# An MoE decoder layer kernel: gated results scattered to their tokens, plain loads in the last stage

## The reference

```python
x1 = _layernorm(x + attn_out, g1, be1)
gate_probs = jax.nn.softmax(x1 @ Wg + bg, axis=-1)
topk_p, topk_i = jax.lax.top_k(gate_probs, K)                 # K = 2 of E = 8
topk_p = topk_p / jnp.sum(topk_p, axis=-1, keepdims=True)
h = jax.nn.gelu(jnp.einsum('bsd,edf->bsef', x1, W1) + b1, approximate=False)
y = jnp.einsum('bsef,efd->bsed', h, W2) + b2
moe_out = sum over the two chosen experts of topk_p * y
return _layernorm(x1 + moe_out, g2, be2)
```

## Time and profile before

| | us |
|---|---|
| median of three runs | 1700.76 |
| lowest, highest | 1695.51, 1703.92 |
| the profiled execution, its own time | 1700.69 |
| its span in the profile | 1698.9 |
| PE, DVE, ACT, POOL busy | 1376.5, 1166.6, 872.7, 642.1 |
| stages one and two end (last scatter issued) | about 1386 |
| tile phase, first to last TensorE work | 1395 to 1566 |
| last stage, first gather to end | 1570 to 1699 |

### The profile page before, as it was taken

How to read it: one execution, slowest core, us unless ns; L and a number is a source line. 1 busy time by engine, 2 the same in 40 slices (tenths; PEclk the granted TensorE clock), 3 DMA queues, 4 the chain that set the end, 5 groups by cost and what they waited for, 6 DMA issues and landing times.

```text
span 1698.9 us, 46753 instructions
## 1 busy us (share of the span) xinstructions
PE 1376.5 (81%) x19192; PEld 1120.8 (66%) x19192; DVE 1166.6 (69%) x3279; ACT 872.7 (51%) x2058; POOL 642.1 (38%) x912
## 2 busy tenths in 40 slices
PE   6899999999859988988989899898997739998000
PEld 5788787888737766766767667676675528887000
DVE  4777887778666888877878787888887631100565
ACT  3556555665425765556566565665666514444000
POOL 6415335243052245433443525535223220000885
PEclk8899999999979999999999999999999959999555
DMA  9932221211110011000010100101000026665232
GB/s 342 381 99 73 66 69 59 87 58 40 61 50 8 9 27 38 25 22 13 24 33 12 40 11 24 36 12 30 21 8 27 14 93 202 202 202 154 62 90 71
DMA packets 114293, 123.04 MB, mean 72 GB/s; under 512 B 21920, under 2 KB 87456, under 8 KB 113824
## 3 DMA queue, kind: packets, MB, share of 16 engines
q1 hardware_dynamic: 107936, 107.46, 19.6%
q0 software_dynamic: 6144, 12.60, 2.6%
HBM read 65.49 MB, written 54.53 MB: 71 GB/s over the span
## 4 chain that ended last, share of the span: by engine, by line
PE 53%; DVE 24%; POOL 8%; ACT 7%; issue 5%; DMA 1%; SPq 1%; DVEq 0%; POOLq 0%; ACTq 0%
PE bank L1847 6%; PE bank L1714 5%; DVE P L1492 4%; PE bank L2101 4%; DVE gs L1491 4%; PE bank L2094 3%; POOL P L1046 3%; PE bank L1726 3%; PE bank L1699 3%; PE bank L1896 2%; PE bank L1970 2%; PE bank L1885 2%; PE bank L1935 2%; PE bank L1892 2%; PE bank L1908 2%
## 5 line engine op out<-in xcount | busy, mean ns | idle before, releaser
L1166 ACT ACTIVATE P<-P 128x512 f32<-128x512 f32 x256 | 160.1, 630 | 99.9 <-DVE P L1492 98.5
L1491 DVE TENSOR_REDUCE gs<-bank 128x8 f32<-128x512 f32 (+1 forms) x256 | 174.5, 682 | 43.2 <-PE bank L1699 21.3
L1714 PE MATMUL bank<-const,P 128*128 128x128 f32 x1152 | 177.2, 284 | 29.4 <-ACT P L1166 20.8
L1492 DVE TENSOR_TENSOR P<-bank,gs 128x512 f32<-128x512 f32 x256 | 177.1, 692 | 8.8
L1714 PEld LDWEIGHTS bank<-const,P 128*128 128x128 f32 x1152 | 130.5, 143 | 70.0 <-ACT P L1166 42.1
L1847 PE MATMUL bank<-XT,wb 128*128 128x256 f32 x512 | 138.2, 397 | 3.1 <-ACT PT L1077 1.2
L1046 POOL DMA_INDIRECT P<-rows_x,places x64 | 64.6, 1009 | 200.9 <-DMA rows_x<-R 183.4
L1172 ACT ACTIVATE PT<-bank 128x512 f32<-128x512 f32 x192 | 109.7, 594 | 51.1 <-PE bank L1714 49.8
L1649 DVE TENSOR_TENSOR R<-bank,Q 128x256 f32<-128x256 f32 x40 | 17.0, 425 | 164.0 <-PE bank L2101 164.0
L989 POOL TENSOR_TENSOR P<-P,gs 128x512 f32<-128x512 f32 x64 | 66.0, 1046 | 155.4 <-DVE gs L1528 154.9
L1263 ACT ACTIVATE PT<-bank,Q 128x256 f32<-128x256 f32 x160 | 67.4, 471 | 84.7 <-PE bank L2094 84.4
(11 more groups left out here) (264 smaller groups left out, 3564.5 us busy)
## 6 DMA issues: line engine op xcount, KB each, us to landing
Q<-in_wm SPq DMA_DIRECT2D x40, 578.0 KB, 3.8
rows_x<-blank SPq DMA_DIRECT2D x4, 4864.0 KB, 33.7
y_mid<-PT SPq DMA_DIRECT2D x16, 512.0 KB, 2.8
y_mid<-D SPq DMA_DIRECT2D x16, 512.0 KB, 2.8
X<-rows_x SPq DMA_DIRECT2D x40, 128.0 KB, 2.2
rows_x<-R SPq DMA_DIRECT2D x40, 128.0 KB, 2.6
wb<-in_wb SPq DMA_DIRECT2D x1, 4228.0 KB, 15.3
V<-in_ctxT SPq DMA_DIRECT2D x32, 128.0 KB, 3.0
```

Of the source, the lines that this page charges most:

```text
L1166: act.activation(P[s][:, i, :], P[s][:, i, :], ACT.Exp, scale=scale).then_inc(p.of(s), 1)
L1491: st2(dve.tensor_reduce(mx, v, AX.X, ALU.max))
L1492: dve.tensor_tensor(P[s][:, i, :].rearrange("p (g m) -> p g m", m=width), v, each(mx, width), ALU.subtract).then_inc(s_sub.of(s), 1)
L1714: last = pe.transpose(tile(banks[s][i], t), tile(P[s][:, i, :], t), ident)
```

## The change

Rows of `rows_x` grow from 128 to 132 numbers: the token's row number plus one, its first expert, g1 and g2 follow the state. A tile's weights get one more column, the expert's number. X1 becomes a view of the wider buffer XW. In the tile phase DVE works out from these columns, for each row of the tile, the gate that applies and the row of a new DRAM tensor `y_rows` for the result (first choices in one part, second ones in another, rows without a token to spare rows). It multiplies the result by the gate behind the add of b2, and GpSimd scatters it there with two indirect DMAs a tile. SP's store of the tile goes. In the last stage SP loads both results of a group with plain loads, GpSimd adds them, DVE adds x1; the multiplication by g2 is joined with the subtraction of the mean, the one by 1/sqrt with the addition of x; the last normalisation is ACT's. The written-out orders of stages three and four are new (`pool3` and `act4` are added). Steady `sp3` is now "tx" of tile k+1, then "tw" of tile k, and it begins with "tx" of tiles 2, 3, 1, 0 and then "tw" of 0, 1, 2, 3, while TensorE turns tiles 0, 2, 1, 3 before its first up. Steady `dve3` is mostly "tp" of tile k+2, then "ty" of tile k+1. In `pe3` the steps of three tiles are interleaved.

```diff
@@ constants, buffers, lanes
+WIDE = DIM + 4
+PART = SEQ * SEQ + 1
-WM, NWM = spans(("w1", 512), ("w2", 512), ("b1", 4), ("b2", 128))
+WM, NWM = spans(("w1", 512), ("w2", 512), ("b1", 4), ("b2", 128), ("eid", 1))
-        X1 = per_slot("X1", [128, T, DIM])
+        XW = per_slot("XW", [128, T, WIDE])
+        X1 = [XW[s][:, :, 0:DIM] for s in range(SLOTS)]
-        blank = sb("blank", [128, 512])
+        blank = sb("blank", [128, 4 * WIDE])
@@ SP, stages three and four
             def tile(j, s):
                 yield "tx"
                 if j:
                     sp.wait_ge(m_x_ps.of(s), m_x_ps.at(j - 1, s))
+                    sp.wait_ge(m_row.of(s), m_row.at(j - 1, s))
...
-                yield "ty"
-                sp.wait_ge(m_y.of(s), m_y.at(j, s))
-                to = sp.value_load(table[0:1, j * SLOTS + s, 0:1], min_val=0, max_val=XROWS - NT)
-                sp.dma_start(d["rows_x"][bass.ds(to, NT), :].rearrange("(t p) d -> p t d", p=128), R[s][:, :, :]).then_inc(tile_y[s], 16)
...
+            for s in range(SLOTS):
+                sp.wait_ge(m_gelu.of(s), m_gelu.at(ROUNDS - 1, s))
+                sp.wait_ge(tile_y[s], 16 * T * ROUNDS)
+            for s in range(SLOTS):
+                load_results(0, s)
             def finish(n, s):
+                if n + 1 < passes:
+                    yield "ly"
+                    sp.wait_ge(c_ln_mv.of(s), c_ln_mv.at(n, s))
+                    load_results(n + 1, s)
+                    load_last_x1(n + 1, s)
+                    yield "lx"
+                    sp.wait_ge(c_r2_mv.of(s), c_r2_mv.at(n, s))
+                    load_last_x(n + 1, s)
                 yield "out"
@@ POOL, stages three and four
-                        pool.indirect_dma_start(P4[s][:, k, 128 * t:128 * t + 128], None, d["rows_x"][:, :], bass.IndirectOffsetOnAxis(
-                            ap=places[:, (n * SLOTS + s) * T + t, k:k + 1], axis=0)).then_inc(gathered[s], 16)
+            def tile(j, s):
+                yield "sc"
+                pool.wait_ge(m_gated.of(s), m_gated.at(j, s))
+                for t in range(T):
+                    pool.indirect_dma_start(d["y_rows"][:, :], bass.IndirectOffsetOnAxis(
+                        ap=gidx[s][:, t, j % 2:j % 2 + 1], axis=0), R[s][:, t, :], None).then_inc(tile_y[s], 16)
+            def finish(n, s):
+                yield "su"
+                pool.wait_ge(last_y[s], 16 * 3 * (n + 1))
                 if n:
                     pool.wait_ge(c_ln_mv.of(s), c_ln_mv.at(n - 1, s))
+                pool.tensor_tensor(P4[s][:, 2, :], P4[s][:, 0, :], P4[s][:, 1, :], ALU.add).then_inc(c_sum.of(s), 1)
                 yield "n4"
                 root(n, s, c_ln_mv, c_ln_rstd, pool2, 0)
                 yield "n5"
-                root(n, s, c_r2_mv, c_ln_rstd, pool2)
+                pool.wait_ge(c_r2_mv.of(s), c_r2_mv.at(n, s))
+                apart(pool)
+                pool2(pool, pool.tensor_scalar(rstd[s][:, :], mv[s][:, :, 1], EPS, None, ALU.add))
+                pool2(pool, pool.tensor_tensor(rstd[s][:, :], rstd[s][:, :], power[:, 0:T], ALU.pow))
+                pool2(pool, pool.tensor_tensor(shift[s][:, :], mv[s][:, :, 0], rstd[s][:, :], ALU.mult))
+                pool.tensor_scalar(shift[s][:, :], shift[s][:, :], -1.0, None, ALU.mult).then_inc(c_ln_rstd.of(s), 1)
@@ ACT, stage four
+            def finish(n, s):
+                yield "n5"
+                act.wait_ge(c_ln_rstd.of(s), c_ln_rstd.at(n, s, use=1))
+                if n:
+                    act.wait_ge(written[s], 16 * n)
+                for t in range(T):
+                    last = act.activation(X1[s][:, t, :], R[s][:, t, :], ACT.Identity, bias=shift[s][:, t:t + 1], scale=rstd[s][:, t:t + 1])
+                last.then_inc(c_out.of(s), 1)
@@ DVE, place (stage two)
-                g1, g2 = gates[:, c0:c0 + T, 0], gates[:, c0:c0 + T, 1]
+                g1, g2 = XW[s][:, :, DIM + 2], XW[s][:, :, DIM + 3]
+                dve.tensor_scalar(XW[s][:, :, DIM], C("rowbase")[:, c0:c0 + T], 1.0 / NE, 1.0, ALU.mult, ALU.add)
                 dve.wait_ge(b_g_exp.of(s), b_g_exp.at(n, s))
+                dve.tensor_copy(XW[s][:, :, DIM + 1], idf[:, :, 0])
@@ DVE, stages three and four
             def tile(j, s):
+                yield "tp"
+                row, e1, g1, g2 = (XW[s][:, :, DIM + k] for k in range(4))
+                eid = part(wm[s], WM, "eid")
+                dve.wait_ge(tile_x[s], 16 * (j + 1))
+                dve.wait_ge(tile_w[s], 16 * (j + 1))
+                dve.scalar_tensor_tensor(small[s][:, 0, 0:T], e1, eid, g1, ALU.is_equal, ALU.mult)
+                dve.scalar_tensor_tensor(small[s][:, 1, 0:T], e1, eid, g2, ALU.not_equal, ALU.mult)
+                st2(dve.tensor_scalar(small[s][:, 2, 0:T], e1, eid, float(PART), ALU.not_equal, ALU.mult))
+                dve.tensor_tensor(small[s][:, 3, 0:T], small[s][:, 0, 0:T], small[s][:, 1, 0:T], ALU.add)
...
+                dve.tensor_copy(gidx[s][:, :, j % 2], small[s][:, 4, 0:T]).then_inc(m_row.of(s), 1)
                 yield "ty"
                 dve.wait_ge(m_down_ps.of(s), m_down_ps.at(j, s))
                 if j:
-                    dve.wait_ge(tile_y[s], 16 * j)
+                    dve.wait_ge(tile_y[s], 16 * T * j)
                 dve.tensor_tensor(R[s][:, :, :], tok(half(s, 0)), over(part(wm[s], WM, "b2"), T), ALU.add).then_inc(m_y.of(s), 1)
+                dve.wait_ge(m_y.of(s), m_y.at(j, s))
+                for t in range(T):
+                    ins = dve.tensor_scalar(R[s][:, t, :], R[s][:, t, :], small[s][:, 3, t:t + 1], None, ALU.mult)
+                ins.then_inc(m_gated.of(s), 1)
...
+                st2(dve.tensor_tensor(R[s][:, :, :], tok(P4[s][:, 2, :]), tok(lastx1[s]), ALU.add))
                 norm_stats(s, st2, c_ln_mv)
                 yield "n4"
                 y = tok(PT4[s][:, 0, :])
+                dve.wait_ge(c_ln_mv.of(s), c_ln_mv.at(n, s))
+                for t in range(T):
+                    ins = dve.scalar_tensor_tensor(y[:, t, :], R[s][:, t, :], mv[s][:, t, 0:1], Row("g2"), ALU.subtract, ALU.mult)
+                st2(ins)
                 dve.wait_ge(c_ln_rstd.of(s), c_ln_rstd.at(n, s, use=0))
+                dve.wait_ge(last_x[s], 16 * (n + 1))
+                for t in range(T):
+                    ins = dve.scalar_tensor_tensor(R[s][:, t, :], y[:, t, :], rstd[s][:, t:t + 1], tok(lastx[s])[:, t, :], ALU.mult, ALU.add)
                 st2(ins)
                 norm_stats(s, st2, c_r2_mv)
-                yield "n5"
-                if n:
-                    dve.wait_ge(written[s], 16 * n)
-                norm_apply(n, s, c_ln_rstd, c_out, 1, X1[s])
```

More of the change, by code:

```diff
@@ L406 @@
 M_ACT = (("xT", 1), ("gelu", 4))
[L407 to L409 removed]
+M_DVE = (("row", 1), ("y", 1), ("gated", 1))
+C_DVE = (("ln_mv", 1), ("r2_mv", 1))
+C_ACT = (("out", 1),)
+C_POOL = (("sum", 1), ("ln_rstd", 1), ("ln_rstd", 1))
 def in_turn(eng, order, streams):
```

108 lines of the change are left out of this document (55 added, 53 removed), and 50 rows, old and new, of tables (act3, dve3, pe3, sp3).

## The result

| | before | after |
|---|---|---|
| median of 4 runs each, us | 1702.17 | 1642.44 |
| lowest, highest | 1695.51, 1703.92 | 1637.45, 1645.03 |
| the profiled execution, its own time | 1700.69 | 1637.45 |
| its span | 1698.9 | 1635.7 |

The ratio after to before is 0.9653, with a 95% interval from 0.9616 to 0.9689: 59.7 us less by the medians. The forecast was 1656 and its range 1641 to 1676. The result is inside, close to the low end. The profiled execution of after is the shortest of its four, so the two profiles differ by a little more, 63.2 us.

A forecast was written before the change was run, and what follows sets the result against it. It took GpSimd to bound the last stage and TensorE the tile phase. Terms +2.0 +0.5 +3.0 -3.0 -1.5 -46.0 sum to -45.0, taking 1700.69 us to 1656, range 1641 to 1676.

The forecast's parts named there:

- Last stage: Final stage: without gathers, GpSimd and DVE nearly even, 68.2 us from first DVE work to last store for 114.2, -46.0.
- 4.05 us a group: Last stage's pace per group of 256 tokens: 3.63 GpSimd, 3.54 DVE, plus sharing and hand-overs; ends 3.63 and 5.0.
- rival E: Last stage: plain loads come late and hold it at 7 us a group, about 1702 us; chance 0.02.
- Rival A: Last stage: shared SBUF path keeps GpSimd and DVE's two-input instructions apart, 5.0 us a group, 1671 us; chance 0.12.
- Steady tiles: Tile phase: added DVE and GpSimd work hidden beside TensorE, some TensorE idle time gone, -3.0 us, ends -8 and +8.
- Rival C: Tile phase and last stage both better: TensorE's idle time mostly gone (-8), 3.7 us a group, 1645 us; chance 0.10.
- Rival B: Tile phase ten us slower than before, from DVE's added work or scatters and loads disturbing each other, 1669 us; chance 0.15.
- the close turns: Tile phase, `pe3`: in nine of 36 tiles a turn follows the down matmuls by a quarter tile's work; argued for slower tiles.
- Rival D: Tile phase: GpSimd's scatters become its bound, from 2.06 us each; at 3.0 each 1731 us, slower than before; chance 0.03.
- Start of the tile phase: First tiles: four X loads go ahead of the first weights, so TensorE's up starts later, +3.0 us, ends +1 and +4.5.
- The step to the last stage: From the last result add to the last stage: 8.7 us in place of 10.2, -1.5.
- Second stage and clearing: Two more DVE instructions a group in stage two, +2.0 us (0 to +6); wider rows to clear, +0.5 (0 to +1.5).

The follow-up runs named there:

- e4: Changed kernel with four indirect gathers a group on GpSimd in place of the last stage's plain loads, simple regular orders: 1715.89 us, ratio 1.0072.
- e1: Kernel before with only the new tile-phase turn orders of TensorE and ACT (`pe3`, `act3`): 1794.97 us, ratio 1.0596.
- e2: Kernel before with the new `pe3`, `act3` and the new load order `sp3`, SP's store of the result kept: 1689.29 us, ratio 0.9938.
- e3: Changed kernel with the old `pe3` and `act3` of the kernel before: 1659.49 us, ratio 0.9773.
- e6: Changed kernel without DVE's two gate multiplies in the tile phase, gates left out of the result: 1644.15 us, ratio 0.9687.
- e7: Changed kernel with every tile-phase scatter issued twice, the second into a tensor nobody reads: 1694.29 us, ratio 0.9949.

## Why the prediction was right, and where it was off

**The forecast held:** faster, and for the reason given. The last stage was bound by GpSimd's gathers, and e4 shows it from the other side. All but one of the terms came within 5 us of what the profiles show; the steady tiles missed by 13.

**Last stage, -46.0 forecast, -50.0 measured.** The mechanism was right: the two engines nearly even, with a small charge for what they take from each other. The term "4.05 us a group" was 0.15 too large, 3.9 in the middle of the stage. Its parts moved against each other. From start to start GpSimd's pieces are 0.81 + 0.99 + 1.56 = 3.36 (sum, first root, second with shift), where I had 3.63, taking roots from a stage where they came at a slower step. DVE's are 3.20 where I had 3.54, mostly because an aggregate holds DVE for 0.17 and not the 0.30 that I charged, twice. (The 1.56 is the usual; in the round shown above it is 1.77, with a first addition of 0.41.) The wide sum cost 3.4 / 16 = 0.21 and not 0.36. The waits between the engines, charged 0.15, are 5.2 us in 10.2 groups, 0.5. So 3.20 + 0.21 + 0.5 = 3.9. The rest of the 4 us is in filling and finishing: 64.2 - 16 x 3.9 = 1.8, charged 3.4. The loads held a group back only at the start (GpSimd's waits for them are 4.5 us in the whole stage, 4.2 of it for the first): rival E did not occur.

Rival A (the shared path, 5.0 a group) fell, but its row pointed at something that shows again here: the 0.93 for 0.39. It is real beside wide operands, absent beside the narrow power, and rare. (In the earlier trace rows the DVE instruction has one input from SBUF, here two; that the cause is the same is not shown.) The Trainium skill (SBUF — State Buffer, SBUF: two separate sides) calls the path shared by DVE and GpSimd an exclusive lock, for a DVE instruction with two SBUF inputs too. The wide ones above agree: the add of 0.39 that meets the sum ends 0.3 us behind the sum's end, not inside it; beside the power on 128x2 no such wait shows (0.61 for a pair whose usual is 0.61).

**Steady tiles, -3.0 forecast, -16.1 measured.** This is the step that failed. It said that "of the 8.2 us in which TensorE is idle some should go" and gave as the far end "-8 (all idle time gone)". That end was no end, and the term was mis-sized by 13 us. The matmul row's 158.1 us busy is time with a matmul in flight, and one lasts 275 ns where the next can start after some 131 (83.7 us busy for 640 of them after). A TensorE that waits for gelu spends the tail of its last matmul "busy". Between the two windows the idle part fell from 8.2 us in 166.3 to 0.2 in 150, worth some 8 us, and the rest of the gain came out of the busy time. The two rows that held the whole of it were there. One is the wait for gelu, quoted as 13.7 us at the weight load and then set aside as "partly covered": it is 14.1 over the whole window, and 1.2 is left. The other is the weight loads' busy share, 138.6 of 166.3 us before, or 83%, and 138.1 of 150 after, or 92%: it left 0.7 us a tile to gain, 27 us over 39 tiles. The Trainium skill (Perfetto Trace Analysis, Identifying the Most-Contended Engine) says to judge TensorE's headroom not by matmul busy time but by its rate of work and the weight loads' share. The trace agrees with it: by that share an estimate of the far end is -27, with the measured -16 inside.

What caused the gain is settled by e1, e2, e3 and e6: the turn orders remove the wait for gelu, if the order of loads asks for X ahead of them. That second condition was in none of my cases, and without it the same orders cost 96 us.

**Rival C** (better on both, 1645) gives the time that came, and its chance of 0.10 was too low. It was half right in cause: the tiles gained twice its 8 us, while the last stage took 3.9 a group, nearer the forecast's 4.05 than C's 3.7, and 64.2 in all, not "under 60".

**Rival B** (tile phase slower): nothing of it. DVE's `tp` and multiplies are covered (e6), and the close turns cost nothing to be seen. **Rival D**: its threshold of 2.06 us a scatter was for a tile of 4.13 us; at 3.71 it would be 1.86, and the scatters cost 0.96 and stand 1.27 apart. Four of them make the slowdown (e7). The trap of the Trainium skill (SBUF — State Buffer, the "DVE blocks DMA" trap) does not show in their length: the 80 scatters take 953 to 962 ns while DVE is at work for half of the time. But the case hardly tests it: in 37 of 40 tiles GpSimd's first scatter waits for the gate multiplies, and so does not run beside them. The scatters land in 4.0 us where I had charged 2.3; what makes that longer no run tells.

**Start of the tile phase, +3.0 forecast, +3.6 measured,** and nearly as described: the weights are the fifth load at a pitch of 1.16. The 0.5 that I took off for the early turns did not come: in its place the first up waits 0.46 us for ACT's copy, as shown above. **The step to the last stage, -1.5 forecast, -1.3 measured.**

**Second stage and clearing, +2.5 forecast.** The two profiles differ by 0.7, but between the traces of one chip (e1 and e2, e3 and e6) the stage is some 5 us longer, inside the far ends (together 7.5). That may be part of why the medians differ by 3.5 us less than the profiles; it is not shown.

## What to carry to other kernels

Before you price a new order of work on TensorE, add up its waits at the weight loads (not those of the matmuls with them, which are the same gaps) and look at the share of the weight loads; the idle time left beside busy matmuls is no bound of what there is to gain. An order that works further ahead needs its inputs asked for further ahead, and the two go in together or not at all. Where an engine pays for a transfer by the issue, as GpSimd does for an indirect one, move it to a stage in which that engine is idle, and count issues against the new stage's pace: two a tile were free here, four took back the gain.
